# Four-layer cross-attention: the order of semaphore waits on three engines, and two in place of four buffers of shifted scores

## The reference

```python
def L0(x_c, x_s, ...):                    # channels attend over features, 256 x 256 scores a batch
    Mn, Mm = conv1x1(Wn, bn, inorm(x_c)), conv1x1(Wm, bm, inorm(x_s))
    A = softmax(einsum('bct,bcs->bts', Mn, Mm))
    return conv1x1(Wo, bo, einsum('bcs,bts->bct', conv1x1(Wl, bl, x_s), A)) + x_c

def L1(x, ctx, mask, ...):                # L2 is the same with weights of its own
    a = layer_norm(ctx, gamma, beta)
    Q, K, V = heads(x @ Wq.T), heads(a @ Wk.T), heads(a @ Wv.T)      # 16 heads of 16
    attn = softmax(where(mask, Q K^T * 16**-0.5, -inf))
    return x + tanh(gate) * (attn V) @ Wo.T

def L3(x, ctx, ...):                      # one head of 256
    probs = softmax((x @ w_q.T) (ctx @ w_k.T)^T / 16)
    return x + alpha * (probs (ctx @ w_v.T)) @ w_o.T
```

## Time and profile before

| | us |
|---|---|
| median of 3 runs | 609.85 |
| lowest, highest run | 609.54, 612.3 |
| the profiled execution | 612.3 |
| its span, first to last instruction | 610.5 |

### The profile page before, as it was taken

How to read it: one execution, slowest core, us unless ns; L and a number is a source line. 1 busy time by engine, 2 the same in 40 slices (tenths; PEclk the granted TensorE clock), 3 DMA queues, 4 the chain that set the end, 5 groups by cost and what they waited for, 6 DMA issues and landing times.

```text
span 610.5 us, 25738 instructions
## 1 busy us (share of the span) xinstructions
PE 568.1 (93%) x10867; PEld 499.8 (82%) x10867; DVE 469.9 (77%) x1023; ACT 468.9 (77%) x961; POOL 118.2 (19%) x132
## 2 busy tenths in 40 slices
PE   1799999999999999999999999999999999999885
PEld 1678888988798887988889887998889887988774
DVE  5775879787887869778796869878797869876653
ACT  0799879878787779877788769867788778878651
POOL 3603070103310070102501061100601052000000
PEclk9999999999999999999999999999999999999988
DMA  5520001110020100210020100210020100010001
GB/s 144 174 76 2 2 3 45 35 37 2 2 75 3 37 2 4 75 37 2 2 76 2 38 2 3 75 37 2 3 76 2 37 2 3 3 35 4 2 3 34
DMA packets 18500, 18.32 MB, mean 30 GB/s; under 512 B 1829, under 2 KB 18341, under 8 KB 18405
## 3 DMA queue, kind: packets, MB, share of 16 engines
q1 hardware_dynamic: 18024, 16.55, 8.5%
q0 software_dynamic: 320, 0.26, 0.2%
q10 hardware_dynamic: 60, 0.01, 0.0%
HBM read 12.63 MB, written 4.19 MB: 28 GB/s over the span
## 4 chain that ended last, share of the span: by engine, by line
PE 70%; DVE 11%; ACT 10%; issue 5%; DMA 1%; SPq 1%; POOL 0%; DVEq 0%; ACTq 0%; POOLq 0%
PE psum L389 10%; PE psum L728 10%; PE psum L674 9%; PE psum L390 8%; PE psum L391 8%; PE psum L721 5%; DVE negmax L1048 4%; ACT work L849 4%; PE psum L641 4%; PE psum L654 3%; PE psum L544 3%; DVE shifted L1052 2%; ACT v L800 2%; PE psum L453 2%; PE psum L552 1%
## 5 line engine op out<-in xcount | busy, mean ns | idle before, releaser
L849 ACT ACTIVATE work<-shifted 128x512 f32<-128x512 f32 x128 | 79.2, 632 | 19.0 <-DVE shifted L1052 18.5
L1048 DVE TENSOR_REDUCE negmax<-psum 128x8 f32<-128x512 f32 x128 | 87.2, 681 | 7.1 <-PE psum L654 7.1
L1052 DVE TENSOR_TENSOR shifted<-psum,negmax 128x512 f32<-128x512 f32 x128 | 88.5, 691 | 5.2
L863 ACT ACTIVATE work<-psum,group_mask 128x512 f32<-128x512 f32 x128 | 80.5, 697 | 12.6 <-PE psum L674 12.6
L674 PE MATMUL psum<-const,work 64*128 64x64 f32 x1536 | 64.2, 228 | 17.9 <-ACT work L849 14.6
L674 PEld LDWEIGHTS psum<-const,work 64*128 64x128 f32 x1536 | 54.4, 140 | 32.2 <-ACT work L849 20.0
L728 PEld LDWEIGHTS psum<-v,work 128*64 128x64 f32 x2048 | 63.9, 141 | 8.0 <-issue 5.9
L728 PE MATMUL psum<-v,work 128*64 128x34 f32 x2048 | 67.5, 227 | 0.0
L844 ACT ACTIVATE work<-psum,negmax 128x256 f32<-128x256 f32 x128 | 50.3, 512 | 11.4 <-DVE negmax L1044 11.4
L800 ACT ACTIVATE v<-psum 64x256 f32<-64x256 f32 x128 | 49.8, 389 | 11.3 <-PE psum L391 10.0
L792 ACT ACTIVATE kbd<-psum,own_bias,const 128x512 f32<-128x512 f32 x64 | 46.3, 778 | 4.7 <-PE psum L391 4.4
(11 more groups left out here) (181 smaller groups left out, 1536.8 us busy)
## 6 DMA issues: line engine op xcount, KB each, us to landing
x_raw<-in_x_dram SPq DMA_DIRECT2D x8, 512.0 KB, 4.3
c_raw<-in_ctx_dram SPq DMA_DIRECT2D x8, 512.0 KB, 5.0
out_dram<-attn SPq DMA_DIRECT2D x16, 256.0 KB, 2.3
mrow_u<-in_mask_dram SPq DMA_DIRECT2D x8, 64.0 KB, 4.9
kbd<-in_L_xattn_Wq_dram SPq DMA_DIRECT2D x2, 256.0 KB, 6.8
kbd<-in_L_xattn_Wk_dram SPq DMA_DIRECT2D x2, 256.0 KB, 7.1
kbd<-in_L_xattn_Wv_dram SPq DMA_DIRECT2D x2, 256.0 KB, 7.3
kbd<-in_L_xattn_Wo_dram SPq DMA_DIRECT2D x2, 256.0 KB, 8.2
```

What stands on the lines that cost most here:

```text
L849: act.activation(probs[:, exp_row(g, l, i, last), :], shifted[:, i % 4, :], ACT.Exp).then_inc(exps, 1)
L863: act.activation(probsT[:, at, :], o[:], ACT.Copy, scale=group_mask[:, 2 * i + c:2 * i + c + 1]).then_inc(free, 1)
L1048: dve.tensor_reduce(negmax[:, i % 2, :], sv, AX_X, ALU.max, negate=True).then_inc(rowmax, 1)
L1052: dve.tensor_tensor(shifted[:, i % 4, :].rearrange("t (j k) -> t j k", k=C), sv, negmax[:, i % 2, :].unsqueeze(2).broadcast_to([P, NJ, C]) ...
```

## The change

1. `shifted` has two buffers in place of four. VectorE's addition for strip i in layers 1 and 2 waits for the exponential of strip i-2, before for that of strip i-4; in layer 3 for the exponentials two later than before. The transposed weight `wo3T` keeps its place in it.
2. `wait_banks` puts the filled bank's wait first, then `consumed`, then `front`; before it was `front`, `consumed`, `filling`. The lists of `consumed` are in rising order, before in falling order.
3. The T steps of layers 1 and 2, and of layer 3, wait for `exps` behind the banks, before ahead of them.
4. `turn_halves` begins with `pe.sem_inc(pe_held, 1)`.
5. The first scores of layer 1 (`S1.0`) wait for a new semaphore `keys_ready` in place of the `freed` of K1's two banks. ScalarE raises it behind `K1.1`, with a wait for its own copy of `K1.1` to be through.
6. ScalarE's `T1.0` waits for `full`, then for `mask_set`, before the other way round. VectorE's `PV` waits for its own bank first, before last.

```diff
-        shifted = sb("shifted", [P, 4, 512])
+        shifted = sb("shifted", [P, 2, 512])
@@ wait_banks
+                for f, before in ([(filling, 1)] if filling else []) + [(f, 0) for f in consumed]:
+                    bk, n = fill(at, f[:3], last, *f[3:])
+                    need[bk] = max(need.get(bk, 0), released(bk, n - before))
                 for f in front:
...
-                for f, before in [(f, 0) for f in consumed] + ([(filling, 1)] if filling else []):
-                    bk, n = fill(at, f[:3], last, *f[3:])
-                    need[bk] = max(need.get(bk, 0), released(bk, n - before))
@@ proj_step (PE)
-                used = {"O1": [("P", "AT1", i)], "O2": [("P", "AT2", i)], "PV": [("T", 3, 1), ("T", 3, 0)]}.get(name, [])
+                used = {"O1": [("P", "AT1", i)], "O2": [("P", "AT2", i)], "PV": [("T", 3, 0), ("T", 3, 1)]}.get(name, [])
-                    used = [("A", int(name[2]), 2 * i + q) for q in (1, 0)]
+                    used = [("A", int(name[2]), 2 * i + q) for q in range(2)]
@@ scores_step (PE)
-                        front = [("P", "K1", 1), ("P", "K1", 0), ("P", "Q1", 0)]
+                        front = [("P", "Q1", 0)]
...
+                    if l == 1 and i == 0:
+                        pe.wait_ge(keys_ready, g + 1)
@@ turn_halves
+                pe.sem_inc(pe_held, 1)
@@ turn_step (PE), layers 1 and 2; layer 0 and 3 likewise
-                    pe.wait_ge(exps, 18 * g + (8 * (l - 1) + 4 * (i // 2) + 4))
                     o, signal = start_fill(g, step, last)
                     o2, signal2 = start_fill(g, step, last, 1)
+                    pe.wait_ge(exps, 18 * g + (8 * (l - 1) + 4 * (i // 2) + 4))
@@ weighted_step (PE)
-                used, front = [("T", l, i, 1), ("T", l, i, 0)] if l else [("T", 0, n, 0) for n in (i + 1, i) if i % 2 == 0], ()
+                used, front = [("T", l, i, 0), ("T", l, i, 1)] if l else [("T", 0, n, 0) for n in (i, i + 1) if i % 2 == 0], ()
@@ proj_step (ACT), K1
+                    if l == 1 and i:
+                        bk, n = fill(g, step, last)
+                        act.wait_ge(free, released(bk, n))
+                        act.sem_inc(keys_ready, 1)
@@ scores_step (DVE)
-                    if l == 2 or i >= 4:
-                        dve.wait_ge(exps, 18 * g + (8 * (l - 1) + i - 3))
+                    if l == 2 or i >= 2:
+                        dve.wait_ge(exps, 18 * g + (8 * (l - 1) + i - 1))
```

More of the change, by code:

```diff
@@ L246, in build @@
         negmax0 = sb("negmax0", [P, GB, 2])
-        shifted = sb("shifted", [P, 4, 512])
-        wo3T = shifted[:, 0:2, 0:D]
+        shifted = sb("shifted", [P, 2, 512])
+        wo3T = shifted[:, :, 0:D]
         probs = work[:, 0:8, :]
@@ L312, in build @@
         m_hi, ctx_hi, kv_ready = sem("m_hi"), sem("ctx_hi"), sem("kv_ready")
-        own_bias_ready, ident_ready = sem("own_bias_ready"), sem("ident_ready")
+        own_bias_ready, ident_ready, keys_ready = sem("own_bias_ready"), sem("ident_ready"), sem("keys_ready")
         bias_step, o_product_ready = sem("bias_step"), sem("o_product_ready")
@@ L682, in turn_step @@
                         return
+                    o, signal = start_fill(g, step, last, consumed=[("S", 0, i)])
                     o2, signal2 = start_fill(g, ("T", 0, i + 1), last, consumed=[("S", 0, i + 1)])
-                    o, signal = start_fill(g, step, last, consumed=[("S", 0, i)])
                     turn_halves((o, o2), (signal, signal2),
@@ L695, in turn_step @@
                 else:
+                    o, signal = start_fill(g, step, last)
                     pe.wait_ge(exps, 18 * g + (17 + i))
-                    o, signal = start_fill(g, step, last)
                     pe.transpose(o[:, 0:P], probs3[:, 2 * i:2 * i + 2, :].rearrange("t q s -> t (q s)"), ident).then_inc(signal, 1)
@@ L848, in exp_step @@
                     act.wait_ge(freed[bk], released(bk, n))
-                    act.activation(probs[:, exp_row(g, l, i, last), :], shifted[:, i % 4, :], ACT.Exp).then_inc(exps, 1)
+                    act.activation(probs[:, exp_row(g, l, i, last), :], shifted[:, i % 2, :], ACT.Exp).then_inc(exps, 1)
                 else:
@@ L857, in turn_step @@
                 for c in range(2 if l in (1, 2) else 1):
-                    if l == 1 and i == 0 and c == 0:
-                        act.wait_ge(mask_set, g + 1)
                     o, free = filled(g, step, last, c)
@@ L862, in turn_step @@
                     if l in (1, 2):
+                        if l == 1 and i == 0 and c == 0:
+                            act.wait_ge(mask_set, g + 1)
                         act.activation(probsT[:, at, :], o[:], ACT.Copy, scale=group_mask[:, 2 * i + c:2 * i + c + 1]).then_inc(free, 1)
@@ L1028, in proj_step @@
                 elif name == "PV":
+                    o, free, _ = filled(g, step, last)
                     for pp in range(2 if i == 0 else 0):
@@ L1032, in proj_step @@
                     dve.wait_ge(recip_ready, 10 * g + 10)
-                    o, free, _ = filled(g, step, last)
                     for pp in range(2):
@@ L1048, in scores_step @@
                     dve.tensor_reduce(negmax[:, i % 2, :], sv, AX_X, ALU.max, negate=True).then_inc(rowmax, 1)
-                    if l == 2 or i >= 4:
-                        dve.wait_ge(exps, 18 * g + (8 * (l - 1) + i - 3))
+                    if l == 2 or i >= 2:
+                        dve.wait_ge(exps, 18 * g + (8 * (l - 1) + i - 1))
                     dve.wait_ge(rowmax, 18 * g + (8 * l - 8 + i + 1))
-                    dve.tensor_tensor(shifted[:, i % 4, :].rearrange("t (j k) -> t j k", k=C), sv,
+                    dve.tensor_tensor(shifted[:, i % 2, :].rearrange("t (j k) -> t j k", k=C), sv,
                                       negmax[:, i % 2, :].unsqueeze(2).broadcast_to([P, NJ, C]),
@@ L1057, in scores_step @@
                     dve.tensor_reduce(negmax[:, i, 0:2], sv, AX_X, ALU.max, negate=True).then_inc(rowmax, 1)
-                    dve.wait_ge(exps, 18 * g + (13 + i))
+                    dve.wait_ge(exps, 18 * g + (15 + i))
                     dve.wait_ge(rowmax, 18 * g + (17 + i))
```

## The result

The changed kernel took **616.71 us** (median of 5 runs, 614.16 to 620.38), the kernel before 609.85 us (median of 5). The ratio is **1.0113**, with a 95% interval of 1.0076 to 1.0152. The profiled execution's span is 616.9 us at a mean granted clock of 0.985, where that of before had 610.5 at 0.991.

The account below looks back on a forecast made before the run. TensorE was taken to bound the kernel (70% of the chain), though not alone. 0.65 us a group times seven (4.55), 1.0 for the last group and 0.4 for the prologue, say 6.0, on 609.85 gave 615.9 us; range 611.7 to 618.2.

Parts of the forecast that it names:

- O1's term: Output projections O1.0 and O1.1, waiting for `attnT`'s low part: one hop each, 0.09 us, 0.18 a group, all coming through.
- the last group's: Delays in the final group, with no next group's work beside some steps: 1.0 us in sum.
- What a wait costs by its place: TensorE's waits: one wait instruction between late event and work costs 0.09 us, two cost 0.20 (bounds 0.14 to 0.21).
- T1.0: Layer 1's first transposes, waiting for the exponentials: two hops, 0.20 us a group, all coming through.
- xT: ScalarE's first copy at T1.0, with `full` moved into a register instruction: 0 to 0.09 us a group, taken as 0.06.
- T2.0 by way of VectorE: Layer 2's first transposes: 0.20 us swallowed on TensorE, but 0.10 a group comes through VectorE's late score maximum.
- T2.2: Layer 2 transposes: 0.20 us later on TensorE, but hidden behind ScalarE's copy queue, so nothing.
- T0.4: Layer 0 transposes behind the X0.5 exponentials: of 0.20 us some 0.11 a group is left, and all counts.
- Rival (a): Delays drown on their way, only O1's 0.18 times eight and half of the ends stay: 612.0 us, chance 0.14.
- the prologue's 0.4: Delays before the loop: 0.25 us at group 0's S1.0, 0.15 at T0.6 and A0.4 together, 0.4 in sum.
- (b) to (e): Rivals: all delays show, 619.0, 0.07; buffers bind, 617.1, 0.04; faster weight-load seam, 607.0, 0.03; slow TensorE refill, 618.3, 0.02.
- (e): Rival: TensorE gets matmuls slower after a stall in a wait instruction, at least 2.4 us: 618.3 us, chance 0.02.

Follow-up runs that it names:

- q1: The changed kernel without the extra sequencer instruction `pe.sem_inc(pe_held, 1)` ahead of the transposes; 613.16 us, ratio 1.0063 to the kernel before.
- q5: The changed kernel with the waits of transpose step T1.0 alone as before; 614.52 us, ratio 1.0048 to the kernel before.
- p3: The kernel before with parts 5 and 6 of the change alone (`keys_ready`, ScalarE's and VectorE's order of waits); 610.98 us, ratio 0.9991.
- q2: The changed kernel with the order of waits at the output projections O1 and O2 as before; 615.59 us, ratio 1.0090 to the kernel before.
- q4: The changed kernel with the waits of transpose step T2.0 alone as before; 614.40 us, ratio 1.0056 to the kernel before.
- q3: The changed kernel with the waits of transpose step T2.2 alone as before; 616.18 us, ratio 1.0095 to the kernel before.
- p1: The kernel before with part 1 of the change alone, two buffers of `shifted`; 612.05 us, ratio 1.0012.
- n2: The changed kernel measured once more, unchanged but for a remark behind its last line; 616.66 us, ratio 1.0126 to the kernel before.
- n1: The kernel before measured once more, unchanged but for a remark behind its last line; 612.18 us, ratio 1.0000.
- r3: The kernel before with ScalarE's X1.3 ahead of its V3.0 copy, and the late bank's wait on the weight load at T2.1 and T2.3; 607.09 us, ratio 0.9929.

## Why the prediction was right, and where its terms were off

The sign, the place and the time (615.9 for 616.71) came out, but that the time did is partly luck. The traces show 4.4 to 5.4 us for the whole change, less than the 6.0 forecast, since O1's term was wrong and the last group's too high; what lifts the measured difference to 6.9 stood in no term.

**What a wait costs by its place** was right: 0.04, 0.14 and 0.25 us behind the late event (before, q1, after; forecast from the earlier trace rows as 0.04, 0.14 and 0.24 to 0.25). One thing was mis-sized: these are the starts of the first matmul, which then takes 0.36 us and not 0.39, as at O1.0. By the weight loads, which set what follows, a hop is 0.06 and two are 0.17, where 0.09 and 0.20 were taken.

| term, us a group | forecast | measured |
|---|---|---|
| T1.0 | 0.20 | 0.17 at the step; 0.22 to 0.28 in the stretch (q5) |
| xT | 0.06 | 0.07 to 0.10 (p3) |
| O1.0, O1.1 | 0.18 | 0 (q2), 0.12 at the steps |
| T2.0 by way of VectorE | 0.10 | 0.09 to 0.15 (q4) |
| T2.1, T2.3 | 0 | 0 |
| T2.2 | 0 | 0 (q3) |
| T0.4 | 0.11 | 0.10 at its start, 0.14 at XN.0 behind it |
| two buffers | 0 | 0 (p1) |
| sum | 0.65 | 0.46 to 0.55 (the stretch) |

**The step that failed is O1's.** It was put down as coming through since VectorE's end of `attnT` releases it, and what came behind on VectorE wasn't followed far enough: the low part of the state runs there beside GpSimd. Rival (a) had this kind of loss in general, but took O1's delay for the one that stays and T1.0's for the one that drowns; it is the other way round. T1.0's delay also moves GpSimd's work, O1's doesn't: GpSimd's instruction starts 21.1 to 21.2 us behind `T1.0` in before, after and q2 alike. T0.4 was at its step as forecast: from S0.4 to T0.4 are 4.09 us before (460.32 to 464.41) and 4.19 after (464.00 to 468.19).

**The ends.** The last group was put at 1.0 and has 0.4 to 0.7; PV's idle time grew by 0.20, as forecast. In the prologue S1.0 waits 0.89 us; before it is 0.61 (57.29 us), and 0.25 was forecast for it. The whole of the prologue's 0.4 can't be told from its start, which differs by up to 1 us from run to run.

**What stood in no term** are TensorE's stops, and the level of the kernel before. From the first group's `T1.0` to the eighth's, stops included, after takes 492.8 us and n2 492.1, before and n1 488.4: 3.7 to 4.4 us. With 0.4 to 0.7 of the last group and 0.3 of the prologue that is 4.4 to 5.4 us. The stops are nearly 1 us of it in after, and next to nothing in n2, which has fewer of them. The medians differ by 6.9 and 6.7, but the median of before lay between 609.85 and 611.98 in four batches, and both comparisons were made with the low ones; against 611.98 both would be 4.7 us. So the rest of 1.3 us or more is of the size of what before differs by from batch to batch, and its cause stays open; the interval of the ratio is wider too (4.6 to 9.3 us). Of the rivals, (b) to (e) fell: T2.2 doesn't pay, the buffers don't bind, no seam gives anything back, and `T1.0`'s 32 matmuls take 1.22 us behind their stall as before (1.21), so the refill isn't slow. The 62 ns a matmul that the Trainium skill gives ("TensorE: Matmul & The Clock Gate", step-by-step section), weighed beside (e), would be 2.0 us for these 32 (an estimate), and no row here shows it.

## What to carry to other kernels

Of an instruction's waits, let the engine's own instruction hold the one that ends last; each wait instruction between the late event and the work costs 0.10 us or so even where it waits for nothing, in every group. Follow a delay, or a gain, to the next place where two engines meet before it is put in a sum: where the later partner is another one, it ends there (O1 here, T2.2, and r3's T2.1). And an idle time ahead of the bounding engine is worth more than the waits around it: moving one exponential ahead of one copy gave 0.30 us a group, where waits put in their best order gave 0.06 at two steps and nothing in the end.

## What the runs showed of the hardware

- A wait instruction of TensorE's sequencer that is ready costs 0.11 us if it stands behind one that was late (q1 beside after).
- An addition of two SBUF operands on VectorE that starts 0.14 to 0.30 us behind a GpSimd instruction of 1.21 us takes 0.79 to 0.96 us and ends 1.09 to 1.11 us behind that one's start; one that starts 0.54 us or more behind takes its 0.68 (before, after, q2).
- TensorE can stop for 0.2 to 0.8 us with no wait there, at the same instruction in program after program. In one that differs only in which instruction holds the waits (q1) it stops at another place. Nearly all such stops end 2.2 to 3.0 us after a 16 KB packet of instructions was asked for.
- The granted clock fell to half for 3 to 10 us at a time in the last group of all fourteen traces. The kernel before had spans of 606.9 to 611.9 us, so that one execution's span says little below 0.5%.
